# A recommendation tower with table look-ups: where one-hots read their row numbers, how many tables are picked by matmul, how pair sums are moved, and where layer 1 stands

## The reference

```python
e = stack([tbl_f[ids[:, f]] for f in range(26)], axis=1)     # 512 x 26 x 128
sd = einsum('bfd,bd->bf', e, dense)
ss = einsum('bfd,bgd->bfg', e, e)                            # upper triangle: pairs
h = concatenate([dense, sd, pairs, dense], axis=1)           # 512 x 607
h = maximum(h @ W_top1 + b_top1, 0)                          # 607 x 512
h = maximum(h @ W_top2 + b_top2, 0)                          # 512 x 256
y = h @ W_top3                                               # 256 x 1
```

## Time and profile before

| | us |
|---|---|
| median of 3 runs | 146.29 (146.14 to 149.38) |
| the profiled execution | 145.72 |
| its span in the trace | 143.9 |
| busy: PE 108.4, POOL 82.6, DVE 65.0, ACT 61.4 | |
| gathers: 68 on POOL, from 2.77 to 104.9 | |
| picks on PE end | about 53.8 |
| first gram starts | 54.35 |

### The profile page before, as it was taken

One profiled execution on the slowest core, in us unless ns is written; L12 is line 12 of the kernel. 1 busy time (PEld: TensorE's weight loads), 2 busy tenths in 40 slices (PEclk: granted clock), 3 DMA queues, 4 the chain that ended last, 5 costly groups with the idle time before them and its releaser, 6 DMA issues.

```text
span 143.9 us, 1888 instructions
## 1 busy us (share of the span) xinstructions
PE 108.4 (75%) x692; PEld 97.4 (68%) x692; DVE 65.0 (45%) x138; ACT 61.4 (43%) x101; POOL 82.6 (57%) x76
## 2 busy tenths in 40 slices
PE   0007999999999999859509999979950989960792
PEld 0006778887887879758409997879940979950782
DVE  3079759999999934242400544215430013320011
ACT  4205077758997949818401245643320112320011
POOL 4788878998889977777777777777710000000000
PEclk9999999999999999999955999999997579996599
DMA  4999926999893342222232222321121000002000
GB/s 83 338 248 273 305 54 175 315 280 268 223 255 105 91 114 59 55 55 50 66 85 55 59 55 66 85 70 44 50 53 38 0 5 0 0 1 44 10 0 1
DMA packets 8258, 14.86 MB, mean 103 GB/s; under 512 B 4629, under 2 KB 4629, under 8 KB 8250
## 3 DMA queue, kind: packets, MB, share of 16 engines
q1 hardware_dynamic: 5805, 10.21, 25.5%
q0 software_dynamic: 2176, 4.46, 12.3%
q10 hardware_dynamic: 269, 0.09, 0.3%
HBM read 13.96 MB, written 0.00 MB: 97 GB/s over the span
## 4 chain that ended last, share of the span: by engine, by line
POOL 33%; PE 28%; SPq 13%; DMA 10%; issue 9%; DVE 3%; ACTq 2%; ACT 0%
POOL rows L289 33%; SPq L227 13%; PE ps_h_bank L368 12%; PE ps_gram L347 11%; DMA dots<-hot_ids 3%; DMA dots<-table 3%; ACTq L686 2%; DMA rows<-in_tbl,ids_sb 2%; PE ps_h_bank L388 1%; PE ps_dve L330 1%; DMA ids_sb<-in_ids 1%; DVE table L532 1%; DVE hot_ids L532 1%; PE ps_act L330 1%; PE ps_h_bank L400 1%
## 5 line engine op out<-in xcount | busy, mean ns | idle before, releaser
L289 POOL DMA_INDIRECT rows<-in_tbl,ids_sb x68 | 81.8, 1202 | 21.7 <-issue 20.4
L347 PE MATMUL ps_gram<-vecs 128*128 128x108 f32 x256 | 30.7, 276 | 1.1 <-issue 0.9
L498 DVE TENSOR_SCALAR one_hot<-hot_ids,row_id 125x512 fp32r<-125x512 int32 x67 | 27.9, 491 | 7.8 <-DMA hot_ids<-in_hot_ids 6.0
L302 PE MATMUL ps_gram<-one_hot,table_hi 125*128 125x512 f32 x78 | 31.2, 419 | 0.0
L347 PEld LDWEIGHTS ps_gram<-vecs 128*128 128x128 f32 x256 | 29.6, 192 | 1.9 <-issue 1.9
L302 PE MATMUL ps_gram<-one_hot,table_lo 125*128 125x512 f32 x78 | 30.6, 412 | 0.0
L368 PE MATMUL ps_h_bank<-dots,w_dots 128*128 128x128 f32 x96 | 17.6, 359 | 16.8 <-DMA dots<-hot_ids 10.0
L368 PEld LDWEIGHTS ps_h_bank<-dots,w_dots 128*128 128x128 f32 x96 | 16.4, 267 | 17.5 <-DMA dots<-table 7.2
L302 PEld LDWEIGHTS ps_gram<-one_hot,table_lo 125*128 125x128 f32 x78 | 15.5, 199 | 3.9
L302 PEld LDWEIGHTS ps_gram<-one_hot,table_hi 125*128 125x128 f32 x78 | 15.2, 200 | 3.4
L489 DVE COPY vecs<-ps_dve 128x512 f32<-128x512 f32 (+1 forms) x10 | 9.2, 923 | 14.9 <-PE ps_dve L330 14.9
(11 more groups left out here) (36 smaller groups left out, 83.6 us busy)
## 6 DMA issues: line engine op xcount, KB each, us to landing
table<-in_tbl SPq DMA_DIRECT2D x6, 448.0 KB
hot_ids<-in_hot_ids SPq DMA_DIRECT2D x3, 768.0 KB, 5.1
table<-in_tbl SPq DMA_DIRECT2D x3, 560.0 KB
rows<-in_tbl,ids_sb POOLq DMA_INDIRECT x68, 2.6
w_dots<-in_w_dots SPq DMA_DIRECT2D x3, 256.0 KB, 3.5
w_dense<-in_w_dense SPq DMA_DIRECT2D x2, 256.0 KB, 5.8
...
```

What stands on the lines that cost most here:

```text
L289: pool.indirect_dma_start(out=rows[:, t % ROW_SETS, k, :], out_offset=None, in_=ins[f"tbl_{f}"], in_offset=bass.IndirectOffsetOnAxis(ap=id ...
L302: return pe.matmul(ps_pick[:, i % 2, :], part[0:KP, i % PART_RING, k, :], one_hot[0:KP, i % HOT_RING, k, :], start=(part is table_hi and k ...
L347: last = pe.matmul(ps_gram[:, part % 2 * BANKS + g // PER_BANK, c0:c0 + COLS], vecs[:, t % 2, p0:p0 + QUADS, :], vecs[:, t % 2, p0:p0 + QU ...
L498: nc.vector.tensor_scalar(one_hot[0:KP, i % HOT_RING, k, :], hot_ids[0:KP, i, :], row_id[0:KP, at + k:at + k + 1], None, ALU.is_equal).the ...
```

## The change

Seven things are changed.

1. `row_id` is copied to PSUM (`ps_row_id`), and DVE compares two steps in one `tensor_tensor` (`RUNS_DVE`: ids broadcast over the steps, row numbers from PSUM broadcast over the samples), where it compared one step in a `tensor_scalar` with both in SBUF.
2. Table 8 is no longer picked: eight tables are (68 steps for 78), and 18 per tile are gathered. A tile's last batch has two slots. ACT makes the last two steps of every table, the first one too.
3. The ids come in groups of 1, 3 and 4 tables (before: 3, 3 and 3). The second group is issued before table 2, and the small vectors (`b1`, `b2`, `w3`) after table 3.
4. In `sums` and `dots` the 384 elements of a strip's row are contiguous on either side; before, they were four runs of 96. In PSUM the samples of a Gram part lie 128 columns apart, not 108.
5. The dense transposes stand behind `pick(0)`, and transposes of tiles 0 and 1 stand one pick earlier or between other picks.
6. `layer_1_act(t)` and `layer_1_dve(t)` stand behind all four parts of `gram(t + 1, ...)`, where they stood between its second and its fourth; layers 2 and 3 follow them. For tiles 1 and 2 they stand ahead of the Gram after that, together with `layer_1_dense(t)`.
7. The orders on DVE and ACT (`relu_1`, `relu_2`, `read_y`, `read_transposed`) follow those on PE; these parts of the diff are left out below.

```diff
@@ -30,9 +30,12 @@
...
 
-KS_ACT = [[] if i == 0 else [KTS[i] - 1] if KTS[i] == 8 else [KTS[i] - 2, KTS[i] - 1] for i in range(NHOT)]
-KS_DVE = [[k for k in range(KTS[i]) if k not in KS_ACT[i]] for i in range(NHOT)]
-TABLE_RING, PART_RING, HOT_RING, IDS_GROUP = 3, 2, 2, 3
+KS_ACT = [[KTS[i] - 2, KTS[i] - 1] for i in range(NHOT)]
+RUNS_DVE = [[(k, k + 2) for k in range(0, KTS[i] - 2, 2)] for i in range(NHOT)]
+TABLE_RING, PART_RING, HOT_RING = 3, 2, 2
+
+IDS_GROUPS = [(0, 1), (1, 4), (4, NHOT)]
+IDS_GROUP_OF = [n for n, (i0, i1) in enumerate(IDS_GROUPS) for _ in range(i0, i1)]
 EARLY = 1 + NHOT
@@ -97,8 +101,8 @@
...
         sums = [x[0:SLOTS].rearrange(order)[:, 0:QUADS * SLOTS * LANES].bitcast(F32).rearrange(
-                    "a (s b g) -> a s b g", s=QUADS, b=SLOTS)
-                for x, order in ((hot_ids, "a i n -> a (i n)"), (table, "a r k d -> a (r k d)"))]
+                    "a (q s j g) -> a q s j g", q=STRIPS, s=QUADS, j=STEPS)
+                for x, order in ((hot_ids_all, "a n -> a n"), (table, "a r k d -> a (r k d)"))]
 
@@ -183,16 +189,16 @@
...
 
-            src = ps_gram[PITCH * s:PITCH * s + SLOTS, part % 2 * BANKS:(part % 2 + 1) * BANKS, 0:PER_BANK * COLS]
-            dst = sums[t % 2][:, s, :, part * PER_PART:(part + 1) * PER_PART]
-            return (dst.rearrange("a b (k g) -> a b k g", k=BANKS),
-                    src.rearrange("a k (g s b) -> a s b k g", g=PER_BANK, s=QUADS)[:, s])
+            src = ps_gram[PITCH * s:PITCH * s + SLOTS, part % 2 * BANKS:(part % 2 + 1) * BANKS, :].rearrange(
+                "a k (g c) -> a (k g) c", g=PER_BANK)[:, :, SLOTS * s:SLOTS * (s + 1)]
+            return (sums[t % 2][:, :, s, :, part * PER_PART:(part + 1) * PER_PART],
+                    src.rearrange("a g (q j) -> a q j g", q=STRIPS))
 
...
             n = STRIP_ROWS[q]
-            return (dots[STRIP_AT[q]:STRIP_AT[q] + n, t].rearrange("p s j g -> p s (j g)"),
-                    sums[t % 2][0:n, :, STEPS * q:STEPS * (q + 1), :].rearrange("a s j g -> a s (j g)"))
+            return (dots[STRIP_AT[q]:STRIP_AT[q] + n, t].rearrange("p s j g -> p (s j g)"),
+                    sums[t % 2][0:n, q].rearrange("a s j g -> a (s j g)"))
 
@@ -232,28 +238,26 @@
...
                          ).then_inc(s_dense, 16)
+            load_hot_ids(1)
+            sp.wait_ge(s_hi, 1)
+            load_table(2)
+            sp.wait_ge(s_hi, 2)
+            load_table(3)
             sp.dma_start(b1[:, :], ins["b_top1"]).then_inc(s_small, 16)
...
             sp.dma_start(w3[:, :], ins["W_top3"]).then_inc(s_small, 16)
-            sp.wait_ge(s_hi, 1)
-            load_table(2)
-            sp.wait_ge(s_hi, 2)
-            load_hot_ids(1)
-            load_table(3)
+            load_hot_ids(2)
             sp.wait_ge(s_hi, 3)
             load_table(4)
+            weight_piece(0, w1_dense[:, 0, :], ins["w1_dense"][:, 0, :])
             sp.wait_ge(s_hi, 4)
-            load_hot_ids(2)
             load_table(5)
-            weight_piece(0, w1_dense[:, 0, :], ins["w1_dense"][:, 0, :])
+            weight_piece(1, w1_dense[:, 1, :], ins["w1_dense"][:, 1, :])
             sp.wait_ge(s_hi, 5)
             load_table(6)
-            weight_piece(1, w1_dense[:, 1, :], ins["w1_dense"][:, 1, :])
+            dots_piece(2, 0)
             sp.wait_ge(s_hi, 6)
             load_table(7)
-            dots_piece(2, 0)
-            sp.wait_ge(s_hi, 7)
-            load_table(8)
             dots_piece(3, 1)
@@ -306,8 +310,9 @@
...
                         pe.wait_ge(s_hot_act, steps_made(KS_ACT, i, KS_ACT[i].index(k) + 1))
-                    else:
-                        pe.wait_ge(s_hot_dve, steps_made(KS_DVE, i, KS_DVE[i].index(k) + 1))
+                    for n, (k0, _) in enumerate(RUNS_DVE[i]):
+                        if k == k0:
+                            pe.wait_ge(s_hot_dve, steps_made(RUNS_DVE, i, n + 1))
                     products(k, table_hi)
@@ -343,7 +348,7 @@
...
                     p0 = QUADS * (part * PER_PART + g)
-                    c0 = g % PER_BANK * COLS
+                    c0 = g % PER_BANK * P
                     last = pe.matmul(ps_gram[:, part % 2 * BANKS + g // PER_BANK, c0:c0 + COLS],
@@ -400,77 +405,79 @@
...
 
-            pe.wait_ge(s_ident, 1)
-            pe.wait_ge(s_dense, 16)
-            for t in range(TILES):
-                last = pe.transpose(ps_dve[:, t, :], dense[:, t, :], ident[:, :])
-            last.then_inc(s_dense_tp, 1)
+            def dense_transposes():
+                pe.wait_ge(s_ident, 1)
+                pe.wait_ge(s_dense, 16)
+                for t in range(TILES):
+                    last = pe.transpose(ps_dve[:, t, :], dense[:, t, :], ident[:, :])
+                last.then_inc(s_dense_tp, 1)
+
             pick(0)
+            dense_transposes()
             pick(1)
+            transposes(0, 0)
             pick(2)
-            transposes(0, 0)
             transposes(0, 1)
...
             pick(4)
-            pick(5)
             transposes(0, 3)
             transposes(0, 4)
+            pick(5)
+            transposes(1, 0)
             pick(6)
+            transposes(1, 1)
             pick(7)
-            transposes(1, 0)
-            pick(8)
-            transposes(1, 1)
+            transposes(1, 2)
             pe.wait_ge(s_pad, 2)
...
             gram(0, 0)
+            transposes(1, 3)
             gram(0, 1)
-            transposes(1, 2)
             gram(0, 2)
-            transposes(1, 3)
+            transposes(1, 4)
             gram(0, 3)
-            transposes(1, 4)
             layer_1_dense(0)
...
             gram(1, 1)
-            layer_1_act(0)
             transposes(2, 0)
             gram(1, 2)
-            layer_1_dve(0)
             transposes(2, 1)
             gram(1, 3)
+            layer_1_act(0)
+            layer_1_dve(0)
+            transposes(2, 2)
             layer_2(0)
-            transposes(2, 2)
+            transposes(2, 3)
             layer_3(0)
-            transposes(2, 3)
+            layer_1_dense(1)
+            layer_1_act(1)
+            layer_1_dve(1)
             transposes(2, 4)
-            layer_1_dense(1)
+            layer_2(1)
 
             gram(2, 0)
+            layer_3(1)
             gram(2, 1)
-            layer_1_act(1)
             transposes(3, 0)
             gram(2, 2)
-            layer_1_dve(1)
             transposes(3, 1)
             gram(2, 3)
-            layer_2(1)
+            layer_1_dense(2)
             transposes(3, 2)
-            layer_3(1)
-            transposes(3, 3)
-            layer_1_dense(2)
             layer_1_act(2)
             layer_1_dve(2)
+            transposes(3, 3)
+            layer_2(2)
+            layer_3(2)
             transposes(3, 4)
...
             gram(3, 0)
-            layer_2(2)
+            layer_1_dense(3)
             gram(3, 1)
-            layer_3(2)
             gram(3, 2)
             gram(3, 3)
-            layer_1_dense(3)
             layer_1_act(3)
@@ -488,15 +497,17 @@
...
 
-            def one_hots(i, ks):
-                if i % IDS_GROUP == 0 and 0 in ks:
-                    dve.wait_ge(s_hot_ids[i // IDS_GROUP], 16)
-                if i >= HOT_RING and 0 in ks:
-                    dve.wait_ge(s_picked, i - HOT_RING + 1)
-                at = ROW_ID_AT[i]
-                for k in ks:
-                    nc.vector.tensor_scalar(one_hot[0:KP, i % HOT_RING, k, :], hot_ids[0:KP, i, :],
-                                            row_id[0:KP, at + k:at + k + 1], None, ALU.is_equal).then_inc(s_hot_dve, 1)
+            def one_hots(i, n):
+                k0, k1 = RUNS_DVE[i][n]
+                at, shape = ROW_ID_AT[i], [KP, k1 - k0, BATCH]
+                if n == 0:
+                    dve.wait_ge(s_hot_ids[IDS_GROUP_OF[i]], 16)
+                    if i >= HOT_RING:
+                        dve.wait_ge(s_picked, i - HOT_RING + 1)
+                nc.vector.tensor_tensor(
+                    one_hot[0:KP, i % HOT_RING, k0:k1, :], hot_ids[0:KP, i, :].unsqueeze(1).to_broadcast(shape),
+                    ps_row_id[0:KP, at + k0:at + k1].unsqueeze(2).to_broadcast(shape), ALU.is_equal
+                    ).then_inc(s_hot_dve, 1)
 
```

More of the change, by code:

```diff
@@ L112, in build @@
         ps_pick = ps_gram[:, 2:4, :]
+        ps_row_id = ps_h_bank[:, 1, H1 // 2 + P:H1 // 2 + P + sum(STEP_COUNTS)]
         s_ids = sem("s_ids")
         s_dense = sem("s_dense")
-        s_hot_ids = [sem(f"s_hot_ids{n}") for n in range(NHOT // IDS_GROUP)]
+        s_hot_ids = [sem(f"s_hot_ids{n}") for n in range(len(IDS_GROUPS))]
         s_table = [sem(f"s_table{i}") for i in range(NHOT)]
@@ L507, in _ @@
             for i in range(NHOT):
[L508 removed]
+                one_hots(i, 0)
                 low_part(i)
[L510 removed]
+                for n in range(1, len(RUNS_DVE[i])):
+                    one_hots(i, n)
                 if i == 1:
```

61 lines of the change are left out of this document (32 added, 29 removed).

## The result

The changed kernel takes 141.63 us (median of 4 runs, 141.24 to 143.57) against 146.5 beside it: a ratio of 0.967, 95% interval 0.963 to 0.971. It is faster, by 4.9 us and not by the 11 that were forecast; the time lies inside the range. One of the four runs (143.57) was in a slower state of the chip and stands outside the ratio; the ratios further down leave out such runs in the same way. The profiled execution of the changed kernel took 141.24 with a span of 139.4.

The account below looks back on a forecast made before the run. Gathers on GpSimd bound the kernel to about 62.7 us, then strip loops. Picks to gram(0, 0) at 55.1, then Grams, layers and strip trips gave span 132.8; plus 1.8 and 0.6, 135.2. Forecast 135, range 129 to 143.5.

Parts of the forecast that it names:

- I take 0.45: Strip issues on SyncE: with one run of 384 elements per row, each falls from 0.82 to 0.45 us.
- the trip: From a tile's first strip issue to layer 1's start: 8.8 us before, 3.0 less after the change, so 5.8.
- Rival (a): Strip issues stay at 0.82 us, the price of transfers between SBUF partitions: +6.7 us, about 142; chance 0.14.
- the price of the granted clock after it: After TensorE's idling before layer_1(2), 24 products at reduced clock take 5.5 us instead of 2.7.
- (b): PSUM compare frees GpSimd's port only in part: stretch stays 17 us, about 138; chance 0.10.
- (c): Two-operand compares hold GpSimd's gathers off as low parts do: decides from 26 us of stretch, about 152; chance 0.07.
- (d): Picks on VectorE get longer, at 1.5 us a compare: 7 us on everything, 142; chance 0.07.
- the fall of the stretch from 17 to 7: Delay of GpSimd's gathers beyond unhindered pace: 17.4 us before, 7 if PSUM compares free the port and eight low parts remain.
- 8.1 us from nine low parts, about 9 from the compares: Split of the 17.4 us gather stretch before: VectorE's low parts each held one gather; compares then won further rounds.
- minus 4.7 us of TensorE against plus 5.0 of GpSimd: Table 8 no longer picked: 20 products fewer on TensorE, 4.7 us; four gathers more on GpSimd, 5.0 us.
- 5 us of idling: TensorE waiting for tile 2's strips before layer_1(2), with only dense(2) and one transpose to do.

Follow-up runs that it names:

- The run with ScalarE's help: Changed kernel with tile 2's strip issues shared by SyncE (5) and ScalarE (4): 138.85 us, ratio 0.946 to the kernel before.
- the second profile: Profile of the changed kernel run once more with nothing altered: 141.42 us, ratio 0.969 to the kernel before, span 141.1.
- with the relu moved as well: Changed kernel with gram(3) ahead of layer_1(2), layer_1_act(2) ahead of gram(3, 3), and relu_1(2) ahead of ScalarE's strip issues: 128.84 us, ratio 0.876 to the kernel before.

## Why the prediction was right or wrong

The sum stands beside the trace step by step (us from the start of the span):

| step | forecast | measured |
|---|---|---|
| table 1's first compare | 12.6 | 14.93 |
| compare, start to start | 1.23 | 1.13 |
| gram(0, 0) | 55.1 | 55.08 |
| strips(0) leave | 64.2 | 64.03 |
| strips(1) leave | 73.2 | 72.91 |
| layer_1(1) | 80.0 | 81.13 |
| strips(2) leave | 94.3 | 95.62 |
| layer_1(2) | 100.1 | 103.82 |
| gram(3, 0) | 109.6 | 114.01 |
| strips(3) leave | 118.7 | 123.09 |
| layer_1(3) | 122.8 | 128.57 |
| end | 132.8 | 139.4 |

**The step that failed** is, under "Strips", "I take 0.45": the mechanism of the trip was right and its size was not. It measured 0.76 per issue, and the trip 8.2 instead of 5.8. Rival (a), with 0.82 and 142 us, is the case that came, with a chance of 0.14. Of the 6.6 us of span by which the forecast fell short, 0.8 is TensorE's wait for the strips ahead of layer_1(1), 2.4 lie in the trip of tile 2 (8.2 for 5.8) and 1.4 in that of tile 3 (5.5 for 4.1): 4.6. The run with ScalarE's help gave 2.6 to 3.2 back by shortening one of them. The rest is a relu and a copy between layer_1(2) and gram(3) (0.7), layer 1 of tile 3 and its tail (10.8 for 10.0; its 24 products took 5.3 where they took 4.6 before, the granted clock being 0.53 in them for 0.62), and 0.5 of small things. So the 142 of rival (a) is near the 141.6 partly by luck: it put all its 6.7 us on the trips, at 0.82 an issue, and they hold 4.6.

The argument for 0.45 was that a two-row strip costs what a 26-row strip does, so what they share must be the third dimension. They share another thing, that both ends are in SBUF (0.75 and 0.66 us for 26 and 2 rows, against 0.36 and 0.43 out of HBM). The rival's own sentence said so and was given a seventh of the chance.

**Right:** that GpSimd leaves the chain; that compares set the pace of the picks, and that the picks end no earlier than before; gram(0, 0) to 0.02 us, though by two errors that cancel; that TensorE idles before layer_1(2) (7.67 us, though, for 5), and the price of the granted clock after it (5.49 for 24 products, forecast 5.5; 4.64 in the second profile). Rivals (b), (c) and (d) are refuted by the rows: a stretch of 4.7 us and not 17, no gather held by a compare, and 1.13 us a compare and not 1.5.

**Right in mechanism, wrong in credit:** the forecast put the fall of the stretch from 17 to 7 down to the PSUM operand. Alone on the kernel before it takes 17.4 to 3.8, so it is enough; but without it the changed kernel has 8.2 and the kernel before with eight tables 10.9. The size may be decided by how compares from SBUF and gathers fall on each other; that isn't shown. The forecast's "8.1 us from nine low parts, about 9 from the compares" described one trace. Why the compares won 9 us there and less in the other three isn't settled: shorter runs between waits are a candidate that no run isolated.

**Where the gain is.** Eight tables alone give 142.3 on the kernel before, and the whole change 141.6; with nine tables the rest of it gives 147.8. Part 1 alone loses 7.5 us, part 6 gives nothing measurable, part 4 gives 1.4 to 1.7. Parts 3 and 5 were not undone by themselves. The forecast costed part 2 as minus 4.7 us of TensorE against plus 5.0 of GpSimd, and didn't say that it is the one that pays for part 1: the four compares and the low part that go are 5.9 us of the phase that part 1 had lengthened.

**What was not seen at all** is that the order after the change still holds gram(3) behind the strips of tile 2. A Gram stands over the trip of tile 0 alone (TensorE waits 0.35 us behind it); the trip of tile 1 runs beside the layers of tile 0 (0.80), and those of tiles 2 and 3 are open. The forecast wrote "5 us of idling" at that place and priced it, and didn't ask what else in the list could stand there. The rows of tile 3 had landed by 99.5, and the work was gram(3): 10 us, and with the relu moved as well 12.6.
